# Attention scores in two groups of three units instead of three groups of two

## What is computed

```python
h = jnp.maximum(_layernorm(x, axis=-1), 0.0)
q = _heads(h @ Wq + bq); k = _heads(h @ Wk + bk); v = _heads(h @ Wv + bv)
scores = jnp.einsum('bhqd,bhkd->bhqk', q, k) / np.sqrt(HEAD_SIZE)
bias = jnp.where(graph_mask, 0.0, NEG)[:, None]
probs = jax.nn.softmax(scores + bias, axis=-1)
ctx = jnp.einsum('bhqk,bhkd->bhqd', probs, v)
x = x + ctx @ Wf + bf
```

## Time and profile before

| | |
|---|---|
| three runs, us | 592.18, 592.38, 593.95 (median 592.38) |
| profiled execution | 595.3 us, span from the first to the last instruction 593.4 us |
| busy share of the span | PE 97%, PEld 72%, DVE 80%, ACT 87%, POOL 83% |
| chain that ended last | PE 90%, DVE 3%, DMA 2%, ACT 2%, POOL 1%, issue 1% |
| mean granted TensorE clock | 0.991 of full speed |
| longest waits in total | DVE's logits for PE's scores 61.2 us, POOL's split for DVE's cast 41.1 us |

### The profile page before, as it was taken

One profiled execution on the slowest core, in us unless ns is written; L12 is line 12 of the kernel. 1 busy time (PEld: TensorE's weight loads), 2 busy tenths in 40 slices (PEclk: granted clock), 3 DMA queues, 4 the chain that ended last, 5 costly groups with the idle time before them and its releaser, 6 DMA issues.

```text
span 593.4 us, 17728 instructions
## 1 busy us (share of the span) xinstructions
PE 575.9 (97%) x6634; PEld 430.0 (72%) x6634; DVE 476.8 (80%) x1484; ACT 516.4 (87%) x1161; POOL 493.3 (83%) x533
## 2 busy tenths in 40 slices
PE   7997999999999999999999999999999999999986
PEld 7675677777777777777777777777777777777754
DVE  4787888888888888888888888888888888887665
ACT  2597899999999999999999999999999999999982
POOL 2789888888998888899888889988888998888870
PEclk9997999999999999999999999999999999999999
DMA  8047889987879988789998988889988998987863
GB/s 272 8 86 143 126 182 167 169 173 154 161 153 179 166 170 166 169 132 171 180 164 171 161 165 159 154 179 164 173 167 159 154 156 182 162 148 143 127 125 90
DMA packets 277208, 92.41 MB, mean 156 GB/s; under 512 B 259201, under 2 KB 277122, under 8 KB 277122
## 3 DMA queue, kind: packets, MB, share of 16 engines
q1 hardware_dynamic: 275920, 91.26, 80.8%
q10 hardware_dynamic: 1202, 0.01, 0.1%
HBM read 17.05 MB, written 12.58 MB: 50 GB/s over the span
## 4 chain that ended last, share of the span: by engine, by line
PE 90%; DVE 3%; DMA 2%; ACT 2%; POOL 1%; issue 1%; ACTq 0%; POOLq 0%; DVEq 0%
PE ring L1037 20%; PE ring L1039 20%; PE ring L1038 20%; PE scores L1098 12%; PE ctx L1121 5%; PE ring L1133 4%; PE ctx L1123 4%; PE ctx L1122 4%; DMA bf_row<-in_L_gnn_bf_dram 1%; DVE logits L743 1%; PE ring L1163 1%; DVE h_rows L760 1%; ACT qk L567 1%; DMA h_cols<-h_rows 1%; DVE split L767 0%
## 5 line engine op out<-in xcount | busy, mean ns | idle before, releaser
L425 POOL TENSOR_TENSOR p_rows<-probs,p_rows 128x512 f16<-128x512 f32 x190 | 220.4, 1160 | 26.1 <-ACT p_rows L547 25.8
L743 DVE CUSTOM_DVE_ANT_0 logits<-scores,mask,logit_unscale 128x256 f32<-128x256 f32 x384 | 168.9, 477 | 63.1 <-PE scores L1098 61.2
L542 ACT ACTIVATE probs<-logits,raised 128x256 f32<-128x256 f32 x372 | 168.9, 501 | 6.0
L1037 PE MATMUL ring<-h_cols,w_hi 128*128 128x256 f16 x576 | 158.0, 274 | 0.4 <-DMA h_cols<-h_rows 0.4
L1039 PE MATMUL ring<-h_cols,w_lo 128*128 128x256 f16 x576 | 157.9, 274 | 0.0
L1038 PE MATMUL ring<-h_cols,w_hi 128*128 128x256 f16 x576 | 157.8, 274 | 0.0
L411 POOL TENSOR_TENSOR split<-qk,split 128x512 f16<-128x512 f32 x96 | 111.2, 1158 | 41.1 <-DVE split L767 41.1
L547 ACT ACTIVATE p_rows<-probs 128x512 f16<-128x512 f32 x190 | 119.7, 630 | 6.0
L567 ACT ACTIVATE qk<-ring,qk_bias_s,qkv_ratio 128x256 f32<-128x256 f32 x192 | 96.5, 552 | 5.3 <-PE ring L1039 5.3
L1121 PEld LDWEIGHTS ctx<-v_hi,p_cols 128*128 128x128 f16 x756 | 69.2, 97 | 32.5 <-issue 29.9
L1121 PE MATMUL ctx<-v_hi,p_cols 128*128 128x65 f16 x756 | 88.3, 195 | 3.7 <-DVE context L782 3.7
(11 more groups left out here) (116 smaller groups left out, 1156.6 us busy)
## 6 DMA issues: line engine op xcount, KB each, us to landing
x_in<-in_x_dram SPq DMA_DIRECT2D x32, 384.0 KB, 3.8
out_dram<-result SPq DMA_DIRECT2D x62, 192.0 KB, 2.2
p_cols<-p_rows SPq DMA_TRANSPOSE x190, 3.3
adj_in<-in_adj_dram SPq DMA_DIRECT2D x32, 64.0 KB, 2.8
w_raw<-in_L_gnn_Wq_dram SPq DMA_DIRECT2D x1, 576.0 KB, 6.0
w_raw<-in_L_gnn_Wv_dram SPq DMA_DIRECT2D x1, 576.0 KB, 7.8
w_raw<-in_L_gnn_Wf_dram SPq DMA_DIRECT2D x1, 576.0 KB, 8.8
h_cols<-h_rows SPq DMA_TRANSPOSE x30, 4.7
```

Of the source, the lines that this page charges most:

```text
L425: pool.tensor_tensor(p_rows[u][:, 1], probs[u % 3][:], p_rows[u][:, 0], ALU.subtract).then_inc(p_lo_ready, 1)
L542: act.activation(probs[u % 3][:, a], logits[u % 3][:, a], ACT.Exp, bias=raised[u % 3][:, a:a + 1], scale=-1.0).then_inc(probs_ready, 1)
L743: dve.tensor_tensor_reduce(out=logits[u % 3][:, a], in0=score_bank[a][:, u % 2 * S:(u % 2 + 1) * S], in1=mask[b.parity][:, t], scale=logit ...
L1037: pe.matmul(out_ap, a_hi, m_hi, start=first, stop=False)
```

## The change

The scores of a batch now come in two groups of three units, at `attend(0)` and `attend(3)`. Three units of two heads fill the halves of three banks, so the third score bank is the one that was kept for the peaks (`peak_bank = score_bank[2]`). The layout puts a head of unit 0 and a head of unit 2 into the same bank, though they stand in different rows of PE; so the second head of unit 2 waits for `shared_bank_done`, which the last matmul of unit 0's first head sets. Batch 0 keeps three groups, of two, one and three units.

```diff
-    GROUPS = UNITS // 2
+    GROUPS = UNITS // C
...
-        score_bank = [bank("scores0"), bank("scores1")]
-        peak_bank = bank("peaks")
+        score_bank = [bank(f"scores{n}") for n in range(3)]
+        peak_bank = score_bank[2]
...
+        def score_of(u, a):
+
+            n, column = ((1, 0), (2, 0), (0, 0), (2, S), (0, S), (1, S))[u % C * 2 + a]
+            return score_bank[n][:, column:column + S]
...
+        def scored(b, u):
+
+
+            if b.k == 0:
+                return (1, 1, 2, 3, 3, 3)[u]
+            return 3 + (b.k - 1) * GROUPS + u // C + 1
...
-                wait(dve, scores_ready, b.count(GROUPS, u // 2 + 1))
+                wait(dve, scores_ready, scored(b, u))
...
-            def scores(b, g):
-
-                for u in (2 * g, 2 * g + 1):
+            def scores(b, units):
+
+                for u in units:
                     if u < C:
                         wait(pe, qk_hi_ready, b.count(C, u + 1))
                         wait(pe, qk_lo_ready, b.count(C, u + 1))
-                wait(pe, logits_ready, b.count(2 * UNITS, 4 * g))
-                for u in (2 * g, 2 * g + 1):
+                wait(pe, logits_ready, b.count(2 * UNITS, 2 * units[0]))
+                for u in units:
                     t, tile = u // C, split[b.parity][u % C]
                     for n, (q, k) in enumerate(((1, 2), (1, 3), (0, 2))):
                         for a in range(2):
+                            if u % C == 2 and n == 0 and a == 1:
+
+                                wait(pe, shared_bank_done, b.count(GROUPS, u // C + 1))
                             own = slice(D * a, D * a + D)
-                            mm = pe.matmul(score_bank[a][:, u % 2 * S:(u % 2 + 1) * S],
-                                           tile[own, q, t * P:(t + 1) * P], tile[own, k],
+                            mm = pe.matmul(score_of(u, a), tile[own, q, t * P:(t + 1) * P], tile[own, k],
                                            start=(n == 0), stop=(n == 2))
+                            if u % C == 0 and n == 2 and a == 0:
+                                mm.then_inc(shared_bank_done, 1)
                 mm.then_inc(scores_ready, 1)
...
-                    if here and u % 2 == 0:
-                        scores(b, u // 2)
+                    if here and u % C == 0:
+                        scores(b, range(u, u + C))
```

More of the change, by code:

```diff
@@ L201, in gnn_attention @@
         scores_ready = sem("scores_ready")
+        shared_bank_done = sem("shared_bank_done")
         logits_ready = sem("logits_ready")
@@ L493, in cycle @@
                     probs_lo(b, 1)
+                    probs_lo(b, 2)
                 if front:
                     split_lo(b + 1, 0)
-                if here:
-                    probs_lo(b, 2)
+                    add_bias(b + 1)
                 if front:
@@ L503, in cycle @@
                     probs_lo(b, 3)
-                if front:
-                    add_bias(b + 1)
                 if here:
@@ L649, in cycle @@
                     probs_hi(b, 1)
+                if here:
+                    exps(b, 2)
+                    probs_hi(b, 2)
+                if before:
+                    context_hi(b + -1, 0)
                 if front:
@@ L654, in cycle @@
                     h_hi_rows(b + 2)
-                if before:
-                    context_hi(b + -1, 0)
-                if here:
-                    exps(b, 2)
-                    probs_hi(b, 2)
                 if front:
@@ L700, in context_hi_last @@
                 act.activation(ct_hi[1][:, chunks].rearrange("p c q -> p (c q)"),
-                               R_CT[1][:, chunks.start * P:chunks.stop * P], ACT.Copy).then_inc(ct_hi_ready, 1)
+                               ct_of(LAST, 1)[:, chunks.start * P:chunks.stop * P], ACT.Copy).then_inc(ct_hi_ready, 1)
             exps_last(0)
@@ L743, in mask_and_max @@
                     dve.tensor_tensor_reduce(
-                        out=logits[u % 3][:, a], in0=score_bank[a][:, u % 2 * S:(u % 2 + 1) * S],
+                        out=logits[u % 3][:, a], in0=score_of(u, a),
                         in1=mask[b.parity][:, t], scale=logit_unscale[:, 0:1], scalar=FAR,
@@ L936, in cycle @@
                     weights_lo(3, 8)
-                if here:
-                    mask_and_max(b, 2)
+                if before:
+                    context_lo(b + -1, 0)
                 if front:
                     qk_hi_part(b + 1, 0)
-                if before:
-                    context_lo(b + -1, 0)
+                if (b + 3).exists():
+                    layer_stats(b + 3, (0,))
                 if (b + 2).exists():
@@ L1127, in transpose_context @@
                 wait(pe, context_ready, b.count(2, t + 1))
-                if t == 0 and (b + -1).exists():
-                    wait(pe, result_ready, (b + -1).count(2, 2 if b.k < B - 1 else 1))
+                if t == 0 and b.k == B - 1:
+                    pe.wait_ge(logits_ready, b.count(2 * UNITS, 2 * UNITS))
+                elif t == 0 and (b + -1).exists():
+                    wait(pe, result_ready, (b + -1).count(2, 2))
                 if t == 1 and (b + 2).exists():
@@ L1138, in project_out @@
                 wait(pe, ct_lo_ready, b.count(2, t + 1))
-                if t == 1 and b.k < B - 2:
+                if t == 1:
                     wait(pe, result_ready, b.count(2, 1))
+                elif b.k == B - 1:
+                    pe.wait_ge(result_ready, PREV.count(2, 2))
                 for c in range(C):
@@ L1168, in _ @@
             spread_peaks(peak_bank, slice(4, 5))
-            scores(Batch(0), 0)
+            pe.wait_ge(peaks_joined, 2)
+            scores(Batch(0), (0, 1))
             pe.wait_ge(small_in, 64)
@@ L1180, in _ @@
             project_v(Batch(0), 1)
-            scores(Batch(0), 1)
+            scores(Batch(0), (2,))
             project_qk(Batch(1), 0)
             pe.wait_ge(peak_ready, 6)
-            pe.wait_ge(peaks_joined, 2)
-            spread_peaks(peak_bank, slice(5, 6))
+            spread_peaks(ring[1], slice(5, 6))
             project_qk(Batch(1), 1)
+            scores(Batch(0), (3, 4, 5))
             project_qk(Batch(1), 2)
-            scores(Batch(0), 2)
             pe.wait_ge(bf_ready, 1)
@@ L1247, in turn_probs @@
                 else:
-                    pe.wait_ge(logits_ready, LAST.count(2 * UNITS, 2 * UNITS))
+                    pe.wait_ge(logits_ready, LAST.count(2 * UNITS, 2 * UNITS - 2))
                 for a in range(2):
@@ L1266, in project_out_last @@
                 pe.wait_ge(ct_lo_ready, LAST.count(2, nth))
-                pe.wait_ge(result_ready, PREV.count(2, 2))
                 for c in range(chunks.start, chunks.stop):
@@ L1272, in project_out_last @@
                     mm.then_inc(out_ready, 1)
-            scores(LAST, 0)
+            scores(LAST, range(0, C))
             apply_probs(PREV, 2)
@@ L1277, in _ @@
             apply_probs(PREV, 3)
-            scores(LAST, 1)
             transpose_context(PREV, 0)
             apply_probs(PREV, 4)
-            scores(LAST, 2)
+            scores(LAST, range(C, UNITS))
             apply_probs(PREV, 5)
```

32 lines of the change are left out of this document (16 added, 16 removed).

## The result

| | before | after |
|---|---|---|
| median, us | 592.4 (592.18 to 593.95, 4 runs) | 708.95 (708.56 to 709.59, 4 runs) |
| profiled execution, span | 595.3, 593.4 | 709.6, 707.7 |
| mean granted TensorE clock | 0.991 | 0.961 |

The changed kernel takes 1.196 times as long as the one before (95% interval 1.194 to 1.197). 715 us was predicted, 653 to 743 as the range.

The account below looks back on a forecast made before the run. PE bounded the kernel before; the new wait for POOL's split was to make a loop of 20.8 us, 21.5 with clock falls. 28 x (21.5 - 17.31) = 117.3, +4.0, +1.2 gives +122.5 on 592.38: 715 us, range 653 to 743.

Parts of the forecast that it names:

- The bound: Kernel before, batch 2 on: each batch takes 17.31 us, all PE time; in 28 of 30 cycles PE never waits.
- The steps out of and into the score form: PE, each score group: 0.10 us extra in and 0.10 out; one group fewer makes PE's own batch 17.1.
- `shared_bank_done` costs nothing: PE's wait in each group, for a matmul eight places earlier: taken as 0, at most 6 us over 62 groups.
- The loop: Score matmuls through ACT, DVE's h_rows and unit 3's logits to POOL's split of unit 2: next batch starts at 20.8 us.
- the h_rows pair: DVE's two subtractions beside POOL's split and residual: 2.47 us taken; with the steady row's 1.38 a batch would be 19.7.
- Where PE stands: PE's waits: 2 to 4 us before every first score group, released by POOL's split; about 1 before the second V projection.
- The clock: PE's clock falls to half in two batches of three, costing 1.0 us on the score matmuls: 0.7 mean, 21.5 a batch.
- Start-up and end: Batch 2 starts 4.0 us later, as batch 1's first group waits for its third split; cycle 30 +1.2; tail 0.
- the upper bound: Cold start every batch and one cast held up 0.7 us by a POOL operation: 22.5 a batch, 743 us.
- PE stays the bound: Rival: split of unit 2 ends by 17.1 us after the start, so PE still binds; about 588 us, chance 0.05.
- ACT's stream alone: Rival: unit 3's logits early enough, block 3 follows qk_1 directly; 18.1 us a batch, 620 us, chance 0.08.
- a fall of the clock in two places of one batch: Rival: PE becomes the bound at half clock, 22.5 us of PE time a batch; 745 us and more, chance 0.07.

Follow-up runs that it names:

- The six groups: Kernel before with six score groups of one unit instead of three of two; 621.11 us.
- the grouping alone: Changed kernel with its two groups of three, but ACT, DVE and POOL in the order of the kernel before; 639.98 us, 1.079 times before.
- DVE's one exchange: Changed kernel with unit 3's logits and divide(b-1, 1) ahead of the two h_rows subtractions on DVE; 661.45 us.
- the orders alone: Kernel before with its three groups of two, but ACT, DVE and POOL in the changed kernel's order; four runs, 702.32 to 717.61 us.
- the split ahead of the last p_rows: Changed kernel with POOL's split of unit 2 ahead of p_rows of unit 4; 686.29 us.
- the run in which it ended early and DVE's pair was moved: Grouping by three, old orders, except POOL's split of unit 2 ahead of the residual additions and DVE's h_rows ahead of qk_0's cast; 590.60 us, 0.9960 times before.

## Why the prediction was right, point by point

**The bound.** That PE was the only limit before, and that a wait reaching PE would cost its full length, held: in the middle PE is busy for 17.27, and the 3.6 of its waits come on top.

**The steps out of and into the score form.** 184.77 to 184.88 is 0.11, and 184.88 to 185.09 is 0.21: 0.10 extra before the group, as before. Eighteen matmuls take 1.08 to the next one at 186.17, nine pairs of 0.11 and 0.09 extra. No step inside a group stands out (0.02 or less between the two heads of unit 2, as for the other units), so `shared_bank_done` costs nothing, as taken, though the matmul that it waits for stands nine places earlier and not eight. The six groups give the same price in the time.

**The loop.** Each station came within 0.1 us of the sum. The rows answer to the earlier trace rows, counted from 177.03:

```profile
185.44 1.01 ACT L581 ACTIVATE qk<-ring,qk_bias_s,qkv_ratio 128x256 f32<-128x256 f32 x2
...
190.73 0.30 ACT L552 ACTIVATE raised<-least,p_raise 128x2 f32<-128x2 f32 x1 [2.54 <-DVE least L757]
...
192.54 1.00 ACT L581 ACTIVATE qk<-ring,qk_bias_s,qkv_ratio 128x256 f32<-128x256 f32 x2
```

```profile
178.23 0.48 DVE L757 CUSTOM_DVE_ANT_0 logits<-scores,mask,logit_unscale 128x256 f32<-128x256 f32 x1 [2.83 <-PE scores L1111]
...
186.49 0.43 DVE L781 CAST split<-qk 128x512 f16<-128x512 f32 x1 [0.35 <-ACT qk L581]
...
187.30 2.52 DVE L774 SCALAR_TENSOR_TENSOR h_rows<-normed,h_rows 128x384 f16<-128x384 f32 x2
189.75 0.47 DVE L757 CUSTOM_DVE_ANT_0 logits<-scores,mask,logit_unscale 128x256 f32<-128x256 f32 x1
```

```profile
187.00 1.15 POOL L428 TENSOR_TENSOR split<-qk,split 128x512 f16<-128x512 f32 x1 [0.59 <-DVE split L781]
188.11 2.58 POOL L437 TENSOR_TENSOR residual<-x_in,bf_full 128x384 f32<-128x384 f32 x2
...
196.52 1.15 POOL L428 TENSOR_TENSOR split<-qk,split 128x512 f16<-128x512 f32 x1
```

| from the start, us | logits 0 | qk_0 | cast | h_rows | logits 3 | block 3 | qk_2 | split 2 | next start |
|---|---|---|---|---|---|---|---|---|---|
| predicted | 1.20 | 8.45 | 9.49 | 10.29 | 12.76 | 13.75 | 15.56 | 19.47 | 20.8 |
| measured | 1.20 | 8.41 | 9.46 | 10.27 | 12.72 | 13.70 | 15.51 | 19.49 | 20.89 |

The one that could have been sized either way, the h_rows pair, took 2.45 to the next start (2.52 in its row) with POOL's split and residual beside it. Its two halves end at 188.56 and 189.83, 0.41 and 0.42 after POOL's operation beside each (the split ends at 188.15, the first residual addition at 189.41); the Trainium skill's rule on a whole-instruction exclusion ("SBUF — State Buffer", section "Who interferes with whom") holds in this trace. With the grouping alone, where POOL is idle beside most of the pair (172.17 to 173.39, the pair from 172.04 to 173.05), its row is 1.02 long, and much the same in all 28 batches.

**What the prediction blamed.** It gave the loss to the first group's new wait for all three splits. That is one loop, worth 1.45 a batch by itself (18.76). The rest, up to 20.89, comes with the engines' new orders, and it needs no third split: with the old groups they cost as much. DVE's one exchange gives back 1.4 of these 2.1 (19.5); the remaining 0.7, on ACT, POOL and the rest of DVE, was not taken apart. The chain was right, its price was not divided among its causes.

**Where PE stands.** This step failed. The prediction put 2 to 4 us before the first group and 1 us before the second V projection. Measured are 0.81 before the first group and none before the second V projection; the larger wait, 2.81, is before `apply_probs(b, 0)`, which waits for divide(b-1, 1), and divide stands on DVE right behind unit 3's logits. I followed what the split waits for, not who else waits for the logits that were made late. The time did not suffer, as both waits hang on the same loop: that the sum came out in spite of the wrong place is owed to that, not to the reasoning.

**The clock.** The step that was mis-sized. The prediction had a fall in two batches of three, on the score matmuls, for 1.0 each: 0.7 on the mean. It fell in 12 of 28, for 0.77 each: 0.3 on the mean, 10 us less in the sum. In all twelve it begins 14.3 to 15.8 after the start and is over before the score matmuls. One lies here (columns as in the earlier trace rows; the gap before `apply_probs` ended at 212.37):

```profile
211.20:213.49 2.29, 1.12 (x17) 0.89 (x18) 2.26 (x10) 1.80 (x5) 1.22 (x2) 0.98 0.76 141
213.49:216.90 3.41, 3.41 (x23) 2.07 (x22) 3.15 (x11) 2.66 (x7) 2.03 (x3) 0.51 0.85 163
216.90:219.58 2.68, 2.68 (x18) 1.51 (x17) 0.56 (x1) 2.27 (x6) 1.66 (x2) 1.00 0.58 109
```

3.41 us at half speed lose 1.7 us of work, and the 0.81 that PE would have waited anyway takes up about half of it. Where no idle time stands behind it, the full 1.7 shows: 22.37 against 20.68 with the orders alone, and 1.3 to 1.4 there and with the split ahead of the last p_rows, where the fall begins some 0.4 before the gap ends. The warning of the Trainium skill's "TensorE: Matmul & The Clock Gate", section "HAM oscillation — how this bites in real kernels", of a cold restart in every iteration (in an example that waits some 3 to 5 us each time), came true in 12 of 28 here, with a wait of 2.81.

**Start-up and end.** 4.6 against 4.0 (batch 1's first group 49.09 against 48.5), 0.9 against 1.2, 0.3 against 0. In sum the batches were 0.09 longer at full clock than predicted and lost 0.4 less to the clock: 28 x 0.3 is 9 us, which is more than the 6 between 715 and 709; the median of before lay lower under its profiled execution (2.9) than that of after (0.6). In the upper bound, the cast held up was priced at 0.7; its rows give 1.01 - 0.42 = 0.6, which lowers that bound from 743 to 740.

**The rivals.** That PE stays the bound was decided at the right point: the split ended 20.6 after the start, not by 17.1. In the run in which it ended early and DVE's pair was moved, PE did become the bound with two groups, at 17.05. ACT's blocks were parted by unit 3's logits (2.54 idle before block 3), so ACT's stream alone did not set the loop; and a fall of the clock in two places of one batch did not show.

## What to carry to other kernels

When a change merges stages, follow the chain that starts and ends at the merged stage, with every in-order queue that it passes: its length, not the busy shares, is the new time of a round. An instruction moved forward on a side engine stands in that sum in full if the chain passes that engine behind it; taking it out gives back only what the next longest loop leaves (here 1.4 of 2.45). Having found what is late, list everyone who waits for it, not only the one that you came from. Split such a change into its regrouping and its reordering before judging either: here the reordering cost more than the regrouping, and the regrouping paid, by 0.4%, once one wait after the other was taken out of its loop.

## What was not expected of the hardware

- The granted clock fell in 12 of 28 batches although the gap before was 2.81 in each; it fell between 0.2 us before and 1.4 us after PE had resumed, and stayed at half for 3.41 us each time. It also fell in 14 of 28 with the orders alone, and in 5 of 28 with unit 3's logits ahead of h_rows, where the longest wait of PE is 2.1. What tells the 12 from the others is open.
- Going from three groups to two took 0.26 off PE's own batch (17.31 to 17.05), where adding groups costs 0.19 each; the remaining 0.07 is not explained.
- With batches of 17.05 transfers land late at changing places, and pulling one forward made another slower to land. The busy share of the transfer engines does not tell which batch: 0.84 to 0.93 in the seven late ones, 0.75 to 1.06 in the others (transfers are counted where they start, so a batch can exceed 1). Why is open.
